# x transposed on the host and Wq centred on the chip, in a fused cross-attention and mixture-of-experts kernel

## What is computed

```
x1  = x  + tanh(g_xattn) * (softmax((LN(x) Wq) (ctx Wk / 8)^T) (ctx Wv) Wo + bo)
out = x1 + tanh(g_ffn)   * sum over the top 2 of 8 experts e of w_e * (gelu(LN(x1) w1[e] + b1[e]) w2[e] + b2[e])
```

## Time and profile before

| | us |
|---|---|
| median of 3 runs | 323.07 (323.06 to 323.4) |
| the profiled execution | 322.94 |
| its span in the trace | 320.8 |
| TensorE busy | 314.4 |
| VectorE busy | 233.7 |
| ScalarE busy | 164.1 |
| GpSimd busy | 78.8 |

### The profile page before, as it was taken

How to read it: one execution, slowest core, us unless ns; L and a number is a source line. 1 busy time by engine, 2 the same in 40 slices (tenths; PEclk the granted TensorE clock), 3 DMA queues, 4 the chain that set the end, 5 groups by cost and what they waited for, 6 DMA issues and landing times.

```text
span 320.8 us, 5745 instructions
## 1 busy us (share of the span) xinstructions
PE 314.4 (98%) x1881; PEld 272.1 (85%) x1881; DVE 233.7 (73%) x563; ACT 164.1 (51%) x577; POOL 78.8 (25%) x158
## 2 busy tenths in 40 slices
PE   7899999999999999999999999999999999999996
PEld 7887988988999999988788888888887899888896
DVE  1889997978889999999998475466667554442643
ACT  2548555686766668775466254444533442321320
POOL 1325448484455536335600000000000000000000
PEclk9999999999999999999999999999999999999999
DMA  6992000000000017600007250000020000000011
GB/s 224 395 197 4 2 3 0 0 3 3 0 0 3 0 52 246 230 1 0 2 0 263 55 208 1 0 0 0 8 102 24 2 0 2 0 0 0 2 65 65
DMA packets 20765, 17.35 MB, mean 54 GB/s; under 512 B 11068, under 2 KB 16900, under 8 KB 20612
## 3 DMA queue, kind: packets, MB, share of 16 engines
q1 hardware_dynamic: 20464, 16.51, 17.0%
q10 hardware_dynamic: 276, 0.52, 0.5%
HBM read 14.93 MB, written 2.10 MB: 53 GB/s over the span
## 4 chain that ended last, share of the span: by engine, by line
PE 88%; DVE 7%; DMA 2%; issue 1%; ACT 1%; SPq 0%; DVEq 0%
PE ps L1098 26%; PE ps L1100 26%; PE ps L1099 26%; PE ps L1183 4%; DMA xt<-in_x_dram 2%; PE ps L1272 1%; PE ps L1118 1%; DVE mx L850 1%; PE ps L1156 1%; DVE pT_lo L808 1%; PE ps L1214 1%; PE ps L1370 1%; ACT sx L580 1%; DVE stats L729 1%; DVE sm L819 1%
## 5 line engine op out<-in xcount | busy, mean ns | idle before, releaser
L667 ACT ACTIVATE gel<-ps,b1sel 128x512 f32<-128x512 f32 x64 | 43.9, 690 | 95.5 <-PE ps L1100 95.4
L1057 DVE CAST h_hi<-gel 128x512 fp32r<-128x512 f32 x64 | 28.4, 443 | 58.7 <-ACT gel L667 58.5
L580 ACT ACTIVATE sx<-ps,mx 128x64 f32<-128x64 f32 x128 | 38.3, 327 | 27.6 <-DVE mx L850 27.6
L1098 PE MATMUL ps<-yT_hi,w_hi 128*128 128x512 f32 (+1 forms) x128 | 50.5, 395 | 0.0
L1099 PE MATMUL ps<-yT_lo,w_hi 128*128 128x512 f32 (+1 forms) x128 | 50.0, 390 | 0.0
L1100 PE MATMUL ps<-yT_hi,w_lo 128*128 128x512 f32 (+1 forms) x128 | 49.9, 390 | 0.0
L1059 DVE TENSOR_TENSOR h_lo<-gel,h_hi 128x512 fp32r<-128x512 f32 x64 | 44.9, 702 | 2.2
L466 POOL TENSOR_TENSOR sx<-sx,rs 128x512 f32<-128x512 f32 x32 | 33.2, 1058 | 48.0 <-DVE rs L824 47.8
L1098 PE MATMUL ps<-h_hi,w_hi 128*128 128x512 f32 x96 | 38.4, 400 | 0.0
L1100 PE MATMUL ps<-h_hi,w_lo 128*128 128x512 f32 x96 | 37.5, 390 | 0.0
L1099 PE MATMUL ps<-h_lo,w_hi 128*128 128x512 f32 x96 | 37.4, 390 | 0.0
(11 more groups left out here) (145 smaller groups left out, 672.7 us busy)
## 6 DMA issues: line engine op xcount, KB each, us to landing
stage_w<-in_L_ffn_w_dram SPq DMA_DIRECT2D x7, 1024.0 KB, 7.3
out_dram<-xt SPq DMA_DIRECT2D x6, 256.0 KB, 2.5
wqT<-in_L_xattn_Wq_dram SPq DMA_DIRECT2D x2, 512.0 KB, 7.9
wv_sb<-in_L_xattn_Wv_dram SPq DMA_DIRECT2D x2, 512.0 KB, 9.3
wo_sb<-in_L_xattn_Wo_dram SPq DMA_DIRECT2D x1, 1024.0 KB, 13.7
xt<-in_x_dram SPq DMA_DIRECT2D x1, 1024.0 KB, 10.7
stage_w<-in_L_ffn_w_dram SPq DMA_DIRECT2D x2, 512.0 KB, 4.4
wk_sb<-in_L_xattn_Wk_dram ACTq DMA_DIRECT2D x1, 512.0 KB, 4.2
```

The lines of the kernel that those rows point to most:

```text
L580: last = nc.scalar.activation(sx[:, par, c0:c0 + M], ps[:, 2 * par + 1, c0 - BANK:c0 - BANK + M], ACT.Exp, bias=mx[:, par, h:h + 1], accum ...
L667: nc.scalar.activation(gel[:, f % 4, :], ps[:, h_bank, :], ACT.Gelu, bias=b1sel[:, b, slot, f:f + 1]).then_inc(gelu_done, 1)
L1057: nc.vector.tensor_copy(h_hi[:, f % 4, :], gel[:, f % 4, :]).then_inc(hhi_ready, 1)
L1098: mm(acc, hi_w, hi_x, start=start, stop=False)
```

## The change

The kernel gets x a second time, laid out on the host as xT: 128 channels on the partitions, then the tile, the half of the channels, and 128 tokens. It loads it into three tensors xs (tiles 0 to 5, 6 to 13, 14 and 15). xT_hi is a ScalarE copy of that, two steps ahead and triple-buffered, and xT_lo a subtraction on GpSimd. The xn tiles, the x transposes on TensorE and xT_lo on VectorE are gone.

The layer norm's two parts go elsewhere. The mean is taken out of Wq: VectorE sums every row of wqT over the 256 channels and scales by -1/256, and ScalarE (blocks 0, 1 of each half of four) and GpSimd (blocks 2, 3) add that to wqT before the score pairs. The factor rstd becomes the `scale` of the exponentials; the maximum of heads 8 to 15 is multiplied with it by a new VectorE operation (mxs), for which ScalarE waits. x's norm computes no mean, and its Newton refinement is on GpSimd for all tiles: in step -1 (tiles 0 to 3), step 3 (4 to 7), step 6 (8 to 15).

Both vT groups stand ahead of the scores of tile 0 and are copied by ScalarE. A4 moves from bank 0 to bank 7. The loads of x move behind Wq; SP waits for the second kT group before xT's last two parts, and for the last xT_lo before the first expert's weights.

```diff
-        GRP_BANK = dict(zip(groups, [0, 1, 2, 3, 4, 5, 6, 0, 1, 3, 4, 2, 6, 4, 5, 0, 6] + [0, 1] * len(LATE)))
+        GRP_BANK = dict(zip(groups, [0, 1, 2, 3, 4, 5, 6, 7, 1, 3, 4, 2, 6, 4, 5, 0, 6] + [0, 1] * len(LATE)))
-        ACT_READS = [("kT", 0), ("kT", 1), ("vT", 0)]
+        ACT_READS = [("kT", 0), ("kT", 1), ("vT", 0), ("vT", 1)]
+        XT_LOADS = [(0, 2), (2, XS0), (XS0, XS1), (XS1, NT)]
...
             sp.dma_start(ctx_sb[:, :], ctx_tokens.rearrange("b m d -> (b m) d")).then_inc(ld_ctx, 16)
-            load_x(0, 0, 0, 2)
...
-            load_x(1, 0, 2, TB // 2)
             for half in range(2):
                 blocks = slice(half * NP // 2, (half + 1) * NP // 2)
                 sp.dma_start(wqT[:, blocks, :], Wq[:, blocks, :]).then_inc(ld_wq[half], 16)
+            load_x(0, 0, 0, TB // 2)
+            load_xT(0)
...
-            load_x(2, 0, TB // 2, TB)
+            load_xT(1)
...
-            load_x(3, 1, 0, TB)
+            load_x(1, 0, TB // 2, TB)
+            load_x(2, 1, 0, TB)
+
+            sp.wait_ge(grp_done, number[("kT", 1)] + 1)
+            load_xT(2)
+            load_xT(3)
...
+                if q == 0:
+                    sp.wait_ge(xlo_ready, NT)
...
             def step(s, par):
                 if s in (7, 11, 15):
                     y_rstds((s - 7) // 4)
-                t = s + LEAD
-                if active(t) and t != X_BY_DVE:
...
-                    nc.gpsimd.tensor_tensor(xn[:, par, :], tile, mean1[:, ds(t, 1)].broadcast_to([P, D]),
-                                            ALU.subtract).then_inc(xc_ready, 1)
...
                         nc.gpsimd.tensor_tensor(pr, pr, rs[:, q, hs].unsqueeze(2).broadcast_to([P, H // 2, M]),
                                                 ALU.mult).then_inc(mul_done, 1)
-                if s == 1:
-                    newton(*X_PARTS[1], rstd1, ve_x, 2)
-                    pool.sem_inc(x_rstd, 1)
-                if s == 4:
-                    newton(*X_PARTS[2], rstd1, ve_x, 3)
-            pool.wait_ge(guess_ready, 1)
+                if active(s + LEAD):
+                    x_low(s + LEAD)
+                if s in (-1, 3, 6):
+                    x_rstds((-1, 3, 6).index(s))
...
+            def x_low(t):
+
+                pool.wait_ge(xhi_ready, t + 1)
+                nc.gpsimd.tensor_tensor(xT_lo[:, t % XB, :, :], x_raw(t), as_f32(xT_hi[:, t % XB, :, :]),
+                                        ALU.subtract).then_inc(xlo_ready, 1)
+
+            for half in range(2):
+                pool.wait_ge(wq_mean, half + 1)
+                for m in range(4 * half + 2, 4 * half + 4):
+                    last = nc.gpsimd.tensor_tensor(wqT[:, m, :], wqT[:, m, :], wq_off[:, m:m + 1].broadcast_to([P, D]), ALU.add)
+                last.then_inc(wq_pool, 1)
...
-                act.wait_ge(xT_done, t + 1)
-                wait_pos(act, scores_done, t - 1)
-                nc.scalar.activation(xT_hi[:, t % 2, :, :], ps[:, 7, 0:D].rearrange("p (k i) -> p k i", k=KD),
-                                     ACT.Copy).then_inc(xhi_ready, 1)
+                wait_x_raw(act, t)
+                wait_pos(act, scores_done, t - XB + 1)
+                nc.scalar.activation(xT_hi[:, t % XB, :, :], x_raw(t), ACT.Copy).then_inc(xhi_ready, 1)
+
+            def wq_centred(half):
+
+                act.wait_ge(wq_mean, half + 1)
+                for m in range(4 * half, 4 * half + 2):
+                    last = nc.scalar.activation(wqT[:, m, :], wqT[:, m, :], ACT.Identity, bias=wq_off[:, m:m + 1])
+                last.then_inc(wq_act, 1)
 
             group("kT", 0)
+            wq_centred(0)
             group("kT", 1)
-            for g in A0[:7]:
+            wq_centred(1)
+            for g in A0[:6]:
                 group(*g)
             x_high(0)
-            group(*A0[7])
+            x_high(1)
+            for g in A0[6:]:
+                group(*g)
             group("vT", 0)
-            x_high(1)
+            group("vT", 1)
...
-                act.wait_ge(max_done, t + 1)
+                act.wait_ge(mxs_ready, t + 1)
...
-                                                ACT.Exp, bias=mx[:, par, h:h + 1],
+                                                ACT.Exp, bias=mxs[:, par, h - H // 2:h - H // 2 + 1],
+                                                scale=rstd1[:, t:t + 1],
...
+            def wq_means(half):
+
+                blocks = slice(4 * half, 4 * half + 4)
+                dve.wait_ge(ld_wq[half], 16)
+                nc.vector.tensor_reduce(wq_off[:, blocks], wqT[:, blocks, :], AX, ALU.add).then_inc(wq_sum, 1)
+                dve.wait_ge(wq_sum, half + 1)
+                nc.vector.tensor_scalar(wq_off[:, blocks], wq_off[:, blocks], -1.0 / D, None, ALU.mult).then_inc(wq_mean, 1)
...
             group("ctxT", 0)
-            x_stats(0, range(0, 2))
-            x_stats(1, range(2, TB // 2))
-            x_norm(0)
+            for half in range(2):
+                wq_means(half)
+            x_stats(0, range(0, TB // 2))
             dve.wait_ge(tg_spread, 1)
             nc.vector.tensor_copy(tg[:, :], ps[:, 7, 0:2]).then_inc(tg_ready, 1)
-            for g in A0[:6]:
+            for g in A0[:4]:
                 group(*g)
-            x_low(0)
-            for g in A0[6:]:
+            x_norm(0)
+            for g in A0[4:]:
                 group(*g)
-            x_low(1)
-            x_stats(2, range(TB // 2, TB))
...
-                if s == 4:
-                    x_norm(2)
...
-                    nc.vector.tensor_tensor(xT_lo[:, q, :, :], ps[:, 7, 0:D].rearrange("p (k i) -> p k i", k=KD),
-                                            as_f32(xT_hi[:, q, :, :]), ALU.subtract).then_inc(xlo_ready, 1)
...
                     nc.vector.tensor_reduce(mx[:, par, :], sc, AX, ALU.max, negate=True).then_inc(max_done, 1)
+                    dve.wait_ge(max_done, t + 1)
+                    dve.wait_ge(x_rstd, next(i for i, (t0, t1) in enumerate(X_PARTS) if t < t1) + 1)
+                    nc.vector.tensor_scalar(mxs[:, par, :], mx[:, par, H // 2:H], rstd1[:, t:t + 1], None,
+                                            ALU.mult).then_inc(mxs_ready, 1)
...
                 if s == 0:
-                    group("vT", 1)
                     out_bias(0)
-                    x_norm(1)
...
-                if s in (2, 3):
-                    x_stats(3, range(TB + 4 * (s - 2), TB + 4 * (s - 2) + 4))
+                if s == 2:
+                    x_stats(1, range(TB // 2, TB))
+                    x_norm(1)
+                if s in (3, 4):
+                    x_stats(2, range(TB + 4 * (s - 3), TB + 4 * (s - 3) + 4))
+                if s == 5:
+                    x_norm(2)
...
+                pe.wait_ge(wq_act, half + 1)
+                pe.wait_ge(wq_pool, half + 1)
...
-                    for k in range(KD):
-                        last = nc.tensor.transpose(ps[:, 7, k * P:(k + 1) * P], xn[:, q, k * P:(k + 1) * P], ident[:, :])
-                    last.then_inc(xT_done, 1)
...
                 if s == -1:
                     group("vT", 0)
+                    group("vT", 1)
```

More of the change, by code:

```diff
@@ L61, in gated_cross_attention_moe_kernel @@
     stats2 = stats1
-    mean1 = place("mean1", [P, NT])
+    wq_off = place("wq_off", [P, NP])
     rstd1 = place("rstd1", [P, NT])
@@ L75, in gated_cross_attention_moe_kernel @@
     mx = place("mx", [P, 2, H])
+    mxs = place("mxs", [P, 2, H // 2])
     sm = place("sm", [P, 2, H])
@@ L114, in gated_cross_attention_moe_kernel @@
     ctxT = place("ctxT", [P, KD, P], at=first)
+    XS0, XS1 = 6, 14
+    xs = [place("xs0", [P, XS0, KD, P], at=first),
+          place("xs1", [P, XS1 - XS0, KD, P], at=[cursor[0]])]
     first2 = [cursor[0]]
@@ L125, in gated_cross_attention_moe_kernel @@
     yb = place("yb", [P, 2, D], at=first3)
+    xs.append(place("xs2", [P, NT - XS1, KD, P], at=first3))
     assert first3[0] <= first2[0]
@@ L138, in gated_cross_attention_moe_kernel @@
     pT_lo = place("pT_lo", [P, 2, NP, P], f32r, at=second)
-    xT_hi = place("xT_hi", [P, 2, KD, P], f32r, at=second)
-    xT_lo = place("xT_lo", [P, 2, KD, P], f32r, at=second)
-    xn = place("xn", [P, 2, D], at=second)
+    XB = 3
+    xT_hi = place("xT_hi", [P, XB, KD, P], f32r, at=second)
+    xT_lo = place("xT_lo", [P, XB, KD, P], f32r, at=second)
     yT_hi = place("yT_hi", [P, KD, NT * P], f32r, at=second)
@@ L169, in gated_cross_attention_moe_kernel @@
         ld_wk = [sem(f"ld_wk_{i}") for i in range(2)]
-        ld_x = [sem(f"ld_x_{i}") for i in range(4)]
+        ld_x = [sem(f"ld_x_{i}") for i in range(3)]
         ld_g, ld_bo, ld_gate, ld_b12 = sem("ld_g"), sem("ld_bo"), sem("ld_gate"), sem("ld_b12")
@@ L182, in gated_cross_attention_moe_kernel @@
         ln_ready, xc_ready = sem("ln_ready"), sem("xc_ready")
-        xn_ready, xT_done, xhi_ready, xlo_ready = (
-            sem(n) for n in ("xn_ready", "xT_done", "xhi_ready", "xlo_ready"))
```

(34 more changed lines are left out.)

58 lines of the change are left out of this document (16 added, 42 removed).

## The result

The changed kernel takes **342.49 us** (median of 4 runs, 341.7 to 343.17) against 323.06 (4 runs, 322.88 to 323.4): a ratio of 1.0599, 95% interval 1.0567 to 1.0631. That is 19.4 us slower, where 1.7 slower was forecast and 326.9 was the end of the range. The span is 341.0 us, 20.2 longer than before.

A forecast was written before the change was run, and what follows sets the result against it. TensorE and a ScalarE/VectorE ring were taken to run level. Head 0.45, norms 0.5, pT_lo wait 0.2 and GpSimd 2.0 make +3.15, then -1.4: net +1.75, forecast 324.8 us, range 321.9 to 326.9.

The forecast's parts named there:

- The ring: ScalarE and VectorE's loop from one tile's maximum to the next: forecast 6.52 us without y, 6.86 with it.
- The rule: VectorE in two-port mode and GpSimd lock a shared port; applied at y_tile, up to 0.4 us, not counted.
- about half a microsecond of slack between them: Margin between TensorE and the ScalarE/VectorE loop, said to cover that loop being 0.13 us behind per step, steps 8 to 13.
- the ring, not TensorE: Sign that the forecast is wrong: steps 8 to 13 stay at 6.9 us, set by the ScalarE/VectorE loop.
- the slow rival: At the start, late Wq or colliding GpSimd adds make tile 0 1.3 to 2 us later: 326.1 to 326.8, chance 0.17.
- GpSimd's queue: Two Newton refinements in steps 6 and 7 delay tile 6's multiplication; TensorE stands still about 2 us, +2.0 us.
- TensorE: In attention, 16 pairs of x transposes go, 0.215 us each; its steps need 6.49 us, 6.73 with y.
- The head: Start, with Wq's centring: tile 0's scores end near 22.1 us instead of 20.50; +0.45 left at tile 2's maximum.
- The sum: Whole kernel: +3.15 us at the scores of tile 8, then -1.4 to step 15, net +1.75.

The follow-up runs named there:

- second experiment: Kernel before, with maxima of heads 8 to 15 passed through a small VectorE operation (times one) that ScalarE waits for: 328.43 us against 322.93.
- the kernel before with both additions: Kernel before plus a scale column of ones on the exponentials and a maximum scaled by one: 340.5 us against 323.15.

## Why the prediction was wrong

The differences, from each kernel to the one above it, split the 19.4 us:

| | us | step |
|---|---|---|
| changed kernel | 342.49 | |
| without the scale column | 331.97 | -10.5 |
| and without the scaled maximum | 325.39 | -6.6 |
| and with the Newton refinement a step earlier | 321.27 | -4.1 |
| kernel before | 323.06 | +1.8 |

**The ring: the step that failed.** I had 6.86 us for a step with a y transpose; it is 8.08. (The terms that I listed for the ring before add up to 6.91; from maximum to maximum it was 6.94.) Two terms were mis-sized. The scale operand was taken "at nothing (bounds 0 and 0.03 on each of 8; a bias operand is there already)"; it is 0.09 each, 0.74 per tile (from the first exponential at 105.60 to pT_hi at 108.67 it is 3.07, before 2.33). The bounds had no row behind them, and the trace of the kernel before had the row. When the experts' weights are split, ScalarE copies tiles of 128x128 in turn without and with a scale column:

```profile
L650 ACT ACTIVATE w_hi<-stage_w,swt 128x128 fp32r<-128x128 f32 (+1 forms) x48 | 18.8, 392 | 0.0
L647 ACT ACTIVATE w_hi<-stage_w 128x128 fp32r<-128x128 f32 (+1 forms) x48 | 14.5, 302 | 0.0
```

The column is 90 ns there; 8 of it are 0.72 us, and the ring would have come out at 6.86 + 0.72 = 7.6. My reason, that a bias operand is there already, was no bound either: the 0.09 comes on top of the bias. The Trainium skill (ScalarE: Activation LUTs, What ACT_TABLE_LOAD costs) has a sentence for just this: each pointer operand of one column adds about 93 ns to an ACTIVATE. The trace agrees, with 81 ns on the duration and 90 on the spacing. By it, as an estimate, the ring would have been 6.86 + 8 x 0.093 = 7.6 us, 0.9 above TensorE's 6.73.

The scaled maximum was priced 0.20 with bounds 0.15 and 0.3, from a small operation of the norm. From its start to the first exponential it is 113.68 - 112.93 = 0.75. The operation is 0.23 where nothing holds it, near enough to what I took; the rest is the wait for GpSimd's half multiplication. The rule stood in my text, at y_tile, a filler in one step. I did not ask it of the new operation, which has its place in the ring, at a moment at which GpSimd multiplies: the multiplication starts at the reciprocal and lasts 2.04, and reciprocal, yT_lo and maximum leave 0.68 of it (104.86 to 105.54). That xT_lo went away made it worse: with xT_lo between them the hold-up left mxs at 0.38 (second experiment), without it 0.71, so that the 0.28 I had booked as a gain of the ring was given back in full: steps 10 to 13 are 8.07 to 8.09 in the kernel before with both additions, and 8.07 to 8.08 in the changed kernel.

Why that costs 17 us and not less: the text has the ring "level" with TensorE and yet "about half a microsecond of slack between them", which was to cover a ring 0.13 behind. There was no such slack per step: 0.72 added by the scale column in the kernel before made steps 9, 11, 12 and 13 longer by 0.70 to 0.73. So 1.2 us more per tile on the ring has no cover, and 14 to 16 tiles of it are 17 to 19 us. No rival had the ring as its mechanism, although "the ring, not TensorE" stood among the signs; the slow rival was priced at the head alone. That is why the range ended at 326.9.

**GpSimd's queue: right.** The changed kernel, on GpSimd, then what TensorE does:

```profile
69.95 2.04 POOL L485 TENSOR_TENSOR sx<-sx,rs 128x512 f32<-128x512 f32 x2 [7.29 <-DVE rs L868]
71.96 0.73 POOL L500 TENSOR_TENSOR xT_lo<-xs,xT_hi 128x256 fp32r<-128x256 f32 x1
72.65 0.25 POOL L461 TENSOR_SCALAR ve_p<-ve_x 128x8 f32<-128x8 f32 x1
...
76.62 0.23 POOL L461 TENSOR_SCALAR ve_p<-ve_y 128x4 f32<-128x4 f32 x1 [0.20 <-POOL rstd L467]
...
80.49 2.09 POOL L485 TENSOR_TENSOR sx<-sx,rs 128x512 f32<-128x512 f32 x2 [0.18 <-POOL rstd L467]
```
```profile
81.59 0.66 PE L1222 MATMUL ps<-ident,sx 128*128 128x128 f32 x4 [1.76 <-POOL sx L485]
82.63 0.91 PE L1222 MATMUL ps<-ident,sx 128*128 128x128 f32 x4 [0.39 <-POOL sx L485]
```

From multiplication to multiplication it is 10.5 us, where the text has 10.3 (its 10.4 begins 0.1 earlier, and its terms up to the end of the scores add up to 16.0, not 16.1); TensorE stands 2.15 us, text about 2. x_low took 0.73, priced 0.61 with bounds 0.5 and 1.2. Missing was the clock behind a stall: 1.7 us in the kernel without the rstd operations. In the changed kernel it falls twice, the second time here:

```profile
80.00:82.00 2.00, 0.41 (x4) 0.42 (x4) 2.00 (x4) 2.00 (x12) 1.74 (x4) 1.00 0.00 0
82.00:84.00 2.00, 1.61 (x10) 1.37 (x9) 1.13 (x3) 1.44 (x6) 1.27 (x2) 0.72 0.00 0
84.00:86.00 2.00, 2.00 (x6) 1.52 (x6) 1.75 (x4) 1.61 (x7) 0.12 (x1) 0.50 0.00 0
```

**TensorE: right.** Without rstd in the ring and with the queue mended, the y steps take 6.70, text 6.73. (Two pairs are 6.95 - 6.49 = 0.46, where the text has 0.43.)

**The head: right.** Here are, on VectorE, the first reduction of Wq and the maxima of tiles 0 and 2, and on TensorE the score pairs:

```profile
8.14 1.22 DVE L820 TENSOR_REDUCE wq_off<-wqT 128x4 f32<-128x1024 f32 x1 [3.27 <-DMA wqT<-in_L_xattn_Wq_dram]
...
21.90 1.22 DVE L879 TENSOR_REDUCE mx<-ps 128x16 f32<-128x1024 f32 x1 [2.27 <-PE ps L1136]
...
35.51 1.16 DVE L879 TENSOR_REDUCE mx<-ps 128x16 f32<-128x1024 f32 x1
```
```profile
10.98 2.95 PE L1179 MATMUL ps<-kT_sb,wqT 64*128 64x128 f32 x48 [1.44 <-ACT kT_sb L569]
14.16 1.16 PE L1179 MATMUL ps<-kT_sb,wqT 64*128 64x128 f32 x16 [0.23 <-DVE a_lo L800]
```

Wq landed at 8.1, not 8.9, so the first pair starts at 10.98 (text 11.6) and the last where it did before. Tile 0's maximum starts at 21.90, text 22.1. The maximum of tile 2 ends at 36.67, text 34.9; the scale and mxs are in that too, and in the kernel without them it ends at 34.70.

**The sum** of all terms but the two was good: 325.39 for the kernel without them, forecast 324.8. Part of that is luck. At the scores of tile 8 that kernel is 4.1 us late (its maximum starts at 80.34, before at 76.28) where the text has 3.15: the clock (+1.7) was missing, and the other terms came out 0.8 better than I had them. From there to the end it wins back 1.5, text 1.4.

## What to carry to other kernels

Before an operand is added to an instruction that a ring repeats eight times per tile, price the operand. Look for two rows of one shape that differ by it, in any part of the kernel, and where there are none, let the bound be wide: 0.09 us became 10 us here. A small new VectorE operation from SBUF to SBUF was held here until GpSimd's running instruction ended, so ask of each such operation what GpSimd does at that moment; with its source in PSUM it was not held. And where two rings run level, each term of either is worth its full price times the number of tiles, so the rival that names the second ring needs a price and a chance of its own.

## What the runs showed that I had not expected

- A scale operand as a column costs ScalarE 0.08 us in the duration of a 128x64 ACTIVATE beside a bias column (327 to 409 ns) and 0.09 from one start to the next; on the 128x512 exponential, whose scale column is its only one, 683 became 756 ns; a constant scale costs nothing (327).
- The 128x8 operation mxs of VectorE takes 0.23 alone and up to 1.04 us beside GpSimd's multiplication (where it was held, it ended within 0.04 us of the end of one half), and 0.23 beside it when the maximum it reads is in PSUM. The reductions and subtractions of the same ring, which read PSUM, kept their durations (maximum 1.22 before, 1.16 to 1.22 after).
- TensorE's granted clock fell to the 1.2 GHz level after some stalls of about 2 us (twice in the changed kernel, after stalls of 1.93 and 2.15; the mean clock of 0.990 makes that 3.4 us of its span) and not after others: in the changed kernel without the scale, TensorE was busy for 1.54 of the 4 us from 76 to 80, and the clock stayed at 1.00.
